# Gate logits of a mixture-of-experts kernel: two float32 matmuls in two column groups in place of a split pair in one

## The reference, cut to what matters

```
for r in range(R):                                   # R = 4 rounds
    flat = cur.reshape(-1, h)                        # 2048 tokens x 128
    logits = flat @ Wg[r] + bg[r]                    # 4 logits a token
    vals, idx = jax.lax.top_k(logits, TOPK)          # the best 2 of 4
    w = jax.nn.softmax(vals, axis=-1)
    cw = jnp.sum(jax.nn.one_hot(idx, E) * w[..., None], axis=1)
    hmid = jax.nn.gelu(jnp.einsum('nh,ehf->enf', flat, W1) + b1[:, None, :])
    y = jnp.einsum('enf,efh->enh', hmid, W2) + b2[:, None, :]
    cur = cur + jnp.einsum('ne,enh->nh', cw, y)
```

## Time and profile before

| | |
|---|---|
| median of 3 runs | 485.56 us (485.32 to 485.97) |
| the profiled execution's own time | 486.61 us |
| its span, first to last instruction | 484.8 us |
| mean granted TensorE clock | 0.996 |
| TensorE busy | 477.9 us, 99% of the span |
| ScalarE, VectorE busy | 393.9 us (81%), 387.7 us (80%) |

### The profile page before, as it was taken

How to read it: one execution, slowest core, us unless ns; L and a number is a source line. 1 busy time by engine, 2 the same in 40 slices (tenths; PEclk the granted TensorE clock), 3 DMA queues, 4 the chain that set the end, 5 groups by cost and what they waited for, 6 DMA issues and landing times.

```text
span 484.8 us, 7478 instructions
## 1 busy us (share of the span) xinstructions
PE 477.9 (99%) x2270; PEld 397.0 (82%) x2270; DVE 387.7 (80%) x641; ACT 393.9 (81%) x542; POOL 118.7 (24%) x102
## 2 busy tenths in 40 slices
PE   7999999999999999999999999999999999999997
PEld 7998888888888888888888888888888887888885
DVE  4789899999879898988898898889897758554343
ACT  3799988888888888988888888888888888697653
POOL 5796212121212112121222121231313144400000
PEclk9999999999999999999999999999999999999999
DMA  7702702020201102020202012120202000000001
GB/s 209 215 5 88 266 18 89 2 87 3 87 11 76 71 16 87 0 87 0 87 0 87 11 76 82 49 89 0 87 2 87 2 0 0 1 0 1 0 22 69
DMA packets 6986, 26.30 MB, mean 54 GB/s; under 512 B 2226, under 2 KB 2610, under 8 KB 4786
## 3 DMA queue, kind: packets, MB, share of 16 engines
q1 hardware_dynamic: 5826, 21.20, 12.1%
q0 software_dynamic: 528, 3.67, 2.2%
q10 hardware_dynamic: 608, 1.11, 0.8%
HBM read 24.81 MB, written 1.18 MB: 54 GB/s over the span
## 4 chain that ended last, share of the span: by engine, by line
PE 96%; DMA 2%; SPq 1%; issue 0%; DVE 0%
PE bank L505 34%; PE bank L506 34%; PE bank L509 26%; DMA stage<-lora_all 2%; PE bank L594 1%; PE bank L595 1%; PE bank L527 1%; SPq L244 0%; SPq L247 0%; PE bank L540 0%; PE bank L524 0%; SPq L257 0%; DVE x L1276 0%; SPq L345 0%; SPq L344 0%
## 5 line engine op out<-in xcount | busy, mean ns | idle before, releaser
L812 ACT ACTIVATE act_out<-bank,vec 128x512 f32<-128x512 f32 x256 | 165.4, 682 | 41.8 <-PE bank L509 32.6
L1115 DVE TENSOR_TENSOR hid_lo<-act_out,hid_hi 128x1024 fp32r<-128x1024 f32 x128 | 156.6, 1243 | 33.3 <-ACT hid_hi L817 33.2
L817 ACT ACTIVATE hid_hi<-act_out 128x1024 fp32r<-128x1024 f32 x128 | 135.9, 1062 | 8.0 <-PE bank L509 0.2
L468 POOL TENSOR_TENSOR cur<-cur,prod 128x512 f32<-128x512 f32 x48 | 64.9, 1352 | 238.4 <-DVE prod L1126 237.9
L505 PE MATMUL bank<-hid_hi,moe_hi 128*128 128x512 f32 x256 | 99.9, 390 | 0.0
L509 PE MATMUL bank<-hid_hi,moe_lo 128*128 128x512 f32 x256 | 99.7, 390 | 0.0
L505 PE MATMUL bank<-xhi,moe_hi 128*128 128x512 f32 x256 | 99.7, 390 | 0.0
L506 PE MATMUL bank<-hid_lo,moe_hi 128*128 128x512 f32 x256 | 99.7, 389 | 0.0
L506 PE MATMUL bank<-xlo,moe_hi 128*128 128x512 f32 x256 | 99.6, 389 | 0.0
L509 PE MATMUL bank<-xhi,moe_lo 128*128 128x512 f32 x256 | 99.6, 389 | 0.0
L505 PEld LDWEIGHTS bank<-hid_hi,moe_hi 128*128 128x128 f32 x256 | 48.1, 188 | 11.3 <-issue 0.2
(11 more groups left out here) (126 smaller groups left out, 569.9 us busy)
## 6 DMA issues: line engine op xcount, KB each, us to landing
cw_all<-cw_dram SPq DMA_DIRECT2D x16, 1024.0 KB, 4.6
stage<-ffn_w POOLq DMA_DIRECT2D x1, 2304.0 KB, 8.5
cw_all<-moe_w SPq DMA_DIRECT2D x4, 512.0 KB, 10.3
stage<-lora_all SPq DMA_DIRECT2D x5, 160.0 KB, 7.1
x<-x_t POOLq DMA_DIRECT2D x3, 256.0 KB, 7.0
out_t<-x SPq DMA_DIRECT2D x3, 256.0 KB, 2.5
cur<-cond_base ACTq DMA_DIRECT2D x2, 256.0 KB, 3.1
stage<-ffn_w POOLq DMA_DIRECT2D x1, 512.0 KB, 3.8
```

What stands on the lines that cost most here:

```text
L468: pool.tensor_tensor(cur[:, c, :], cur[:, c, :], prod[:, s % 2, :], ALU.add).then_inc(add_done, 1)
L812: act.activation(act_out[:, f // 2, f % 2, :], bank[:, f, :], ACT.Gelu_apprx_tanh, bias=vec[:, V_B1 + e * FC + f:V_B1 + e * FC + f + 1]).t ...
L817: act.activation(hid_hi[:, s % 2, 2 * pr:2 * pr + 2, :], act_out[:, pr, :, :], ACT.Copy)\
L1115: dve.tensor_tensor(hid_lo[:, s % 2, 2 * pr:2 * pr + 2, :], act_out[:, pr, :, :], hid_hi[:, s % 2, 2 * pr:2 * pr + 2, :].bitcast(F32), ALU ...
```

## The change

The float32 product is no longer split. `logits` takes the loaded gate weights of all four rounds as they are (`vec`, 32 columns, of which 16 are gate weights and 16 the bias) and `cur` in float32, once for tokens 0 to 255 into partitions 0 to 31 of the bank, and once for tokens 256 to 511 into partitions 32 to 63. VectorE then works on 64 partitions and 8 blocks; it picks the round's four columns when it adds the bias, which falls together with the old reduction. The row is stored by two DMAs. The split of the gate weights, the copy of the round's weights, `gbias` with its DMA, and one memset are gone. `first_logits` waits for `cur` (`cond_cur`) and not for `xlo` (`xs_done`).

```diff
-BLOCKS = CHUNK // SQ
+GROUPS = 2
+SPAN = CHUNK // GROUPS
+BLOCKS = SPAN // SQ
+GATED_ROWS = GROUPS * SQ
...
-V_N = V_WG + ROUNDS * EXPERTS
+V_GB = V_WG + ROUNDS * EXPERTS
+V_N = V_GB + ROUNDS * EXPERTS
...
-            sp.dma_start(gbias[:], gate_bias.to_broadcast([SQ, ROUNDS * EXPERTS])).then_inc(small_in, 16)
...
-                sp.dma_start(cw_dram[slot:slot + 1, :].rearrange("s (e t) -> (s e) t", t=CHUNK),
-                             cw_row[0:EXPERTS, :])\
-                  .then_inc(cw_stored, 16)
+                for g in range(GROUPS):
+                    sp.dma_start(cw_dram[slot:slot + 1, :].rearrange("s (e t) -> (s e) t", t=CHUNK)
+                                 [:, g * SPAN:(g + 1) * SPAN], cw_row[g * SQ:g * SQ + EXPERTS, :]).then_inc(cw_stored, 16)
...
-            pool.memset(wg_raw[:], 0.0).then_inc(const_done, 1)
...
                 if c == 0:
-                    pe.wait_ge(wg_done, 1)
-                pe.wait_ge(xs_done, c + 1)
+                    pe.wait_ge(small_in, 16)
+                pe.wait_ge(cond_cur, c + 1)
...
-                pe.matmul(bank[0:SQ, at, :], wg_now[:], xhi[:, c, :], start=True, stop=False)
-                pe.matmul(bank[0:SQ, at, :], wg_now[:], xlo[:, c, :], start=False, stop=True).then_inc(logit_done, 1)
+                for g in range(GROUPS):
+                    mm = pe.matmul(bank[g * SQ:(g + 1) * SQ, at, 0:SPAN], vec[:, V_WG:V_WG + SQ],
+                                   cur[:, c, g * SPAN:(g + 1) * SPAN], start=True, stop=True)
+                mm.then_inc(logit_done, 1)
...
-                            if k == CHUNKS:
-                                pe.wait_ge(wg_done, rnd + 2)
...
-                dve.transpose(turned[:].rearrange("p t r -> p (t r)"), bank[0:SQ, gate_bank(c), :]).then_inc(gate_step, 1)
+                dve.transpose(turned[:].rearrange("p t r -> p (t r)"), bank[0:GATED_ROWS, gate_bank(c), 0:SPAN])\
+                   .then_inc(gate_step, 1)
                 dve.wait_ge(gate_step, at + 1)
-                dve.tensor_reduce(gate_logit(c), turned[:, :, 0:2 * EXPERTS].rearrange("p t (k e) -> p t e k", k=2),
-                                  AX_X, ALU.add).then_inc(gate_step, 1)
+                dve.tensor_tensor(gate_logit(c), turned[:, :, bass.ds(EXPERTS * rnd, EXPERTS)],
+                                  vec[0:GATED_ROWS, bass.ds(V_GB + EXPERTS * rnd, EXPERTS)].unsqueeze(1)
+                                  .to_broadcast([GATED_ROWS, BLOCKS, EXPERTS]), ALU.add).then_inc(gate_step, 1)
                 dve.wait_ge(gate_step, at + 2)
-                dve.tensor_tensor(gate_logit(c), gate_logit(c), gbias[:, bass.ds(EXPERTS * rnd, EXPERTS)].unsqueeze(1)
-                                  .to_broadcast([SQ, BLOCKS, EXPERTS]), ALU.add).then_inc(gate_step, 1)
...
-                    if s == EXPERTS + 2 and not last:
-
-                        dve.tensor_copy(wg_now[:], wg[:, bass.ds(rnd + 1, 1), :].rearrange("p r e -> p (r e)"))\
-                           .then_inc(wg_done, 1)
...
-            split_gate()
```

More of the change, by code:

```diff
@@ L76 @@
 Z_ALL = 2 * CHUNKS
-GATE_OPS = 16
-CONSTS = 5 + EXPERTS
-GATE_HALF = 10
+GATE_OPS = 15
+CONSTS = 4 + EXPERTS
+GATE_HALF = 9
 GATED, H1, H2, W3, PROJECT, MIXTURE = range(6)
@@ L112, in adaln_ffn @@
 def adaln_ffn(nc, x_t, batch_ids, cond_base, lora_all, lang_lora, lang_embed,
-              moe_w, vecs, gate_bias, ffn_w, out_t):
+              moe_w, vecs, ffn_w, out_t):
     ctx = ExitStack()
@@ L144, in adaln_ffn @@
         emb = sb("emb", [P, BATCHES], F32)
[L145 to L148, removed]
         ids = sb("ids", [1, 2 * BATCHES], I32)
         blank = sb("blank", [P, P], F32)
[L151 to L162, removed]
+        upper = sb("upper", [GATED_ROWS, EXPERTS, EXPERTS], F32)
+        need = sb("need", [GATED_ROWS, EXPERTS], F32)
+        turned = sb("turned", [GATED_ROWS, BLOCKS, SQ], F32)
+        logit = sb("logit", [GATED_ROWS, BLOCKS, EXPERTS], F32)
+        losses = sb("losses", [GATED_ROWS, BLOCKS, EXPERTS], F32)
+        top = sb("top", [GATED_ROWS, BLOCKS], F32)
+        below = sb("below", [GATED_ROWS, BLOCKS, EXPERTS], F32)
+        below_ch = sb("below_ch", [GATED_ROWS, BLOCKS, EXPERTS], F32)
+        half_gap = sb("half_gap", [GATED_ROWS, BLOCKS, EXPERTS], F32)
+        tanh_gap = sb("tanh_gap", [GATED_ROWS, BLOCKS, EXPERTS], F32)
+        cw_tok = sb("cw_tok", [GATED_ROWS, BLOCKS, SQ], F32)
+        cw_row = sb("cw_row", [GATED_ROWS, SPAN], F32)
         cw_dram = nc.dram_tensor("cw_dram", [2, EXPERTS * CHUNK], F32).ap()
@@ L290, in gate_second @@
         def gate_second(c):
-            return bank[0:SQ, gate_bank(c), 0:BLOCKS]
+            return bank[0:GATED_ROWS, gate_bank(c), 0:BLOCKS]
         def lang_bank(half):
@@ L378, in _ @@
             for slot in range(2):
-                store_gate(slot, slot + 1, None, 16 * slot + 16)
+                store_gate(slot, slot + 1, None, 16 * GROUPS * (slot + 1))
                 sp.wait_ge(moe_lo_done, max(MOE_ORDER.index(EXPERTS * slot + e) for e in range(EXPERTS)) + 1)
@@ L384, in _ @@
                 read = sp.to_reg(16 * pair)
-                counts = [(sp.to_reg(2 * pair + slot + 1), sp.to_reg(32 * pair + 16 * slot + 16),
+                counts = [(sp.to_reg(2 * pair + slot + 1), sp.to_reg(16 * GROUPS * (2 * pair + slot + 1)),
                            sp.to_reg(2 * EXPERTS * pair + EXPERTS * (slot - 1) + ADD0)) for slot in range(2)]
@@ L821, in first_gelu @@
                 if f == 0:
-                    act.wait_ge(small_in, 32)
+                    act.wait_ge(small_in, 16)
                 if f == FC - 1:
@@ L1071, in gate_order @@
                                   upper[:].rearrange("p i j -> p (i j)").unsqueeze(1)
-                                  .to_broadcast([SQ, BLOCKS, EXPERTS * EXPERTS]), ALU.mult).then_inc(gate_step, 1)
+                                  .to_broadcast([GATED_ROWS, BLOCKS, EXPERTS * EXPERTS]), ALU.mult).then_inc(gate_step, 1)
+                dve.wait_ge(gate_step, at + 5)
+                dve.tensor_tensor(below[:], gate_logit(c), top[:].unsqueeze(2).to_broadcast([GATED_ROWS, BLOCKS, EXPERTS]),
+                                  ALU.subtract).then_inc(gate_step, 1)
                 dve.wait_ge(gate_step, at + 6)
-                dve.tensor_tensor(below[:], gate_logit(c), top[:].unsqueeze(2).to_broadcast([SQ, BLOCKS, EXPERTS]),
-                                  ALU.subtract).then_inc(gate_step, 1)
-                dve.wait_ge(gate_step, at + 7)
                 dve.tensor_reduce(gate_wins(c), gate_beats(c), AX_X, ALU.add).then_inc(gate_step, 1)
@@ L1108, in gate_weights @@
                 if not first:
[L1109 removed]
+                    dve.wait_ge(cw_stored, 16 * GROUPS * q)
                 dve.transpose(cw_row[:], cw_tok[:].rearrange("p t r -> p (t r)")).then_inc(cw_turned, 1)
@@ L1344 @@
                                 cols(a[g + "h1_s"]), cols(a[g + "h2_s"]), cols(a[g + "w3_s"]),
-                                a[f + "Wg"].transpose(1, 0, 2).reshape(P, ROUNDS * EXPERTS)], axis=1),
-        "gate_bias": a[f + "bg"].reshape(1, ROUNDS * EXPERTS),
+                                a[f + "Wg"].transpose(1, 0, 2).reshape(P, ROUNDS * EXPERTS),
+                                np.broadcast_to(a[f + "bg"].reshape(1, ROUNDS * EXPERTS), (P, ROUNDS * EXPERTS))], axis=1),
         "ffn_w": np.concatenate([a[g + "w1_w"].T[:, None, :], a[g + "w2_w"].T[:, None, :], down(a[g + "h1_w"]),
```

31 lines of the change are left out of this document (8 added, 23 removed).

## The result

The changed kernel takes 489.64 us (median of 4 runs, 489.13 to 490.24), the kernel before beside it 485.44 (485.25 to 485.97). The ratio is 1.009, with a 95% interval from 1.0078 to 1.0102: 4.2 us slower. The profiled execution took 489.44 us, its span is 487.6, its mean granted clock 1.000.

What follows compares the result with a forecast made beforehand. The prediction took TensorE's queue to bound the kernel. The logits pairs (-0.4 us) and the start (-0.1) summed to -0.5, from 485.56 to 485.1 us, called no change; range 484.5 to 492.4.

Steps and rivals of the forecast that it cites:

- Entering and leaving: TensorE switching into and out of each new logits pair: taken as 0 us, bounds 0 to 0.38 us.
- The second rival: TensorE's array drains before and after each pair: +0.38 us each time, 491.2 us; chance 0.17, one side alone 0.05 more.
- the first rival: At the logits pair, the column groups take turns: 0.87 us a pair, 492.0 us; chance 0.20.
- both rivals together: At the logits pair, column groups taking turns plus a drain at each side: 498.2 us; chance 0.03.
- longest wait: TensorE's longest wait for others, put at 2.3 us for LoRA rows, before 17 us.
- The pair's own price: The new logits pair on TensorE: column groups side by side, 0.44 us against 0.47, -0.4 us over 16.
- the objection that both groups read the same 128 partitions: Doubt about overlap at the logits pair: two column groups must read two streams from the same partitions, which no row has.
- The saving: Gate on VectorE: 1.7 us a chunk, 27 us of its 387.7 busy, none on the path.
- Two stores: SP's second store per chunk adds 0.27 us, covered by 14 us before the broadcast is read: cost 0.
- The start: Program start without SP's `gbias` issue: 0 to 0.2 us gained, 0.1 taken.
- the half clock costs nothing: Half clock granted from 11.2 to 14.4 us, at the start: no cost, as TensorE waits at 15.90 anyway.

Runs made afterwards that it cites:

- bf16_32: The kernel before plus a bfloat16 matmul of zeros over 32 array columns ahead of each pair of logits; 489.67 us, before 485.12.
- one_group: The changed kernel with one column group: one float32 matmul of all 512 tokens into 32 partitions, one store; 496.33 us, before 485.12.
- f32_whole_array: As `one_group`, but the float32 matmul uses 128 weight columns and writes all 128 partitions; 491.44 us, before 485.41.
- pair_twice: The changed kernel with both float32 logits matmuls issued two times at each place, same result; 496.44 us, 6.8 over the changed kernel.
- add_from_psum: The changed kernel, with VectorE first copying the gate columns into the bank, so the bias add has one PSUM input; 489.62 us, before 485.27.
- start_alone: The kernel before with the gate bias as 16 more columns of `vec` and no `gbias` load; 485.49 us, before 485.41.
- two_stores: The kernel before with the gate row stored by two DMAs of half the tokens each; 485.08 us, before 485.27.
- f32_full: The kernel before plus a float32 matmul of zeros over the whole array ahead of each pair of logits; 488.04 us, before 485.12.
- probe_gate_add: The changed kernel with three more VectorE operations, results unused, ahead of the add of the bias; 493.12 us.

## Why the prediction was wrong

**The step that failed** is "Entering and leaving", where it says "I take 0, because L594 is nearest". That term of the sum, put at 0, measures 0.31 us a visit, 16 visits 5.0 us, and with it "no change" became 4.2 us slower. TensorE loses time on both sides of each visit. The start is 0.09 us late, the first record 0.02 longer (404 ns for 379), the last record is followed 0.31 instead of 0.22 us later (the second two start at 51.95 + 0.24 = 52.19, L502 at 52.50), and that one's successor 0.11 late (0.34 for 0.23): 0.09 + 0.02 + 0.09 + 0.11 = 0.31. With the pair's 0.44 for 0.47 that is the 0.28 of the traces. L594 was the nearest row by shape and the wrong one by kind: it is float32r, and over 32 columns float32r doesn't switch anything (`bf16_32`). L540, float32 on a part of the array, was the right neighbour, and the prediction had read its 0.19 a side. It set it aside because of one row that seemed to contradict it, without asking in what else the two rows differ.

**The second rival**, a drain at each side, is what happened. It was priced 0.38 us a visit and 491.2; the real size is 0.31 and 489.64, since entering costs 0.11 and not 0.19. It was given 0.17. That the range held the time is luck: it reached up to 492.4 for the sake of the first rival, which is refuted. Its price of both rivals together, 498.2, should read 498.0, which changes nothing, and TensorE's "longest wait" of 2.3 us is the sum of two, the longer 1.8.

The Trainium skill, "TensorEngine Tiling (Array Packing)", Key Properties, states that a change of tiling mode drains TensorE. Here the runs agree for float32: 4.9 us between `one_group` and `f32_whole_array`. What the prediction made of it ("around L594, with 32 columns of the array, it does not") was wrong about which rows are such a change.

**The pair's own price was right.** Two column groups run fully side by side, 0.01 us apart, 0.43 to 0.44 us a pair (`pair_twice`). The first rival is refuted. The reason given, L540, held, and the objection that both groups read the same 128 partitions has no weight here. "TensorE: Matmul & The Clock Gate", Part 3, of the Trainium skill states such concurrency, and this trace agrees for float32.

**VectorE: right that it costs nothing, wrong in size.** The saving was put at 27 us and VectorE busy at about 360; it fell by 9.7, to 378.0. The transposes (0.26 us each), the four larger operations (0.12 to 0.13), the small ones (0.03) and the reduction (0.28) gave back 26 us, nearly as predicted. The missing term is the add: 16.3 us for 3.5, because it waits for GpSimd. The rest nearly cancels: the dropped operations on the gate weights, which the prediction didn't count, give 2.0 us; `hid_lo` takes 2.3 more (158.9 for 156.6) and `ffn_lo` 2.1 more (10.8 for 8.7). All rows of `ffn_lo`, and the rows of `hid_lo` over 1.3 us, start or run beside an operation of GpSimd, but why they are longer was not tested. About 1 us stays unassigned. `add_from_psum` takes 9.8 us off VectorE again and changes no time, so the cover by TensorE holds.

**The store and the start.** Two stores: nothing, as predicted. The start: 0.1 us of gain predicted, between 0.3 of gain and 0.7 of loss measured, which neither shows nor refutes it. Whether "the half clock costs nothing" holds stays open. Of the 42 executions of the kernel before that name a clock, the two at a mean clock of 0.996 took 486.61 and 486.62, 1.2 over the median; but one of `start_alone` took 486.74 at 1.000. The trace of before is a late one: its first pair of logits starts at 29.71 us, those of `two_stores` and `start_alone`, at full clock up to there, at 28.24 and 28.29. It also waited 2.3 us for LoRA rows against 0.4 and 1.2, and what part of the 1.4 us is the clock's the traces do not tell.

**No version here beats the kernel before.** With no drain the pair would save 0.03 us a visit. Two chunks in one visit would pay the drain once: (0.88 + 0.31) / 2 = 0.60 a chunk against 0.47, an estimate that wasn't run. Float32r in two column groups was not run either.

## What to carry to other kernels

A small matmul of another shape in the middle of a dense stream costs its columns and its seams, the places where it meets its neighbours. Read the seams as distances between starts, from the neighbour ahead to the second one behind, for they appear in no list of waits; a "free" seam of one type says nothing of another type, so ask of the nearest row in what else it differs, and weigh the row that contradicts it. Here one pair alone did not pay for its entry; each further pair in the same visit cost only its own 0.43 us (`pair_twice`).

## What the runs showed of the hardware that was not expected

- Float32 or bfloat16 over 32 columns of the array between products over 128 costs about 0.2 to 0.3 us a visit (0.31 for the pair and for `one_group`, 0.22 and 0.23 for the small zeros), float32r over 32 columns from partition 0 nothing, and a change of type over the whole array nothing (`f32_full`: 0.21 us for two records of 0.112).
- An operation of VectorE with two inputs in SBUF waits until GpSimd's running operation has ended. In the changed kernel L1051 starts at 79.62 and GpSimd's add runs from 79.41 to 80.70; L1051 ends at 80.74. All 16 rows of L1051 start beside such an operation, last 0.77 to 1.13 us, and end 0.05 to 0.06 us after it. With one input in PSUM the add takes 192 ns (`add_from_psum`). A copy from SBUF to SBUF waited likewise (L1054 in `probe_gate_add`), one from SBUF to PSUM did not. The Trainium skill, "GPSIMD Engine Reference", 1. Specifications, states that the two engines share SBUF interfaces and contend where VectorE has two SBUF inputs or runs in a 2-port mode; these runs agree, and put the price at what is left of GpSimd's operation, 0.7 to 1.1 us here. That the copy runs in such a mode no run here shows.

```profile
79.41 1.29 POOL L465 TENSOR_TENSOR cur<-cur,prod 128x512 f32<-128x512 f32 x1 [3.99 <-DVE prod L1122]
79.62 1.12 DVE L1051 TENSOR_TENSOR bank<-turned,vec 64x32 f32 x1
```

- A wait of 2.0 us on TensorE cost 3.5: behind it the granted clock was at half, 1.2 GHz, for most of the time from 36 to 40 us (`probe_gate_add`, one execution). In the trace before, the half clock from 11.2 to 14.4 us likewise stands behind a wait of 1.8 us; in `add_from_psum`, whose longest wait for LoRA rows is 1.0 us, there is no such stretch up to 28 us.
